# Gated cross-attention and mixture-of-experts block on one core: table scatters issued one by one, row statistics moved between the heads, and Wq's low parts made between GpSimd's additions

## The chip, the cores and the metric

One core of a Trainium2 chip runs the whole program in one launch. The metric is device microseconds of one execution.

## What is computed

Cut to what matters (16 sequences of 112 rows, width 512, context of 375 rows of 128; 16 heads; 64 experts, 8 chosen per row):

```python
def attention(hidden_q, kv_c):                     # kv_r = rope(kv_c)
    q_big = einsum(hidden_q @ Wq.T, w_kc_q)        # per head: 512 -> 128 -> 384
    q_big = rope(q_big)
    scores = (q_big @ W_qr) @ (kv_r @ W_kr).T      # softmax over 375
    return concat(softmax(scores) @ kv_r @ w_kc_kv) @ Wo.T

def experts(x):
    topv, topi = top_k(x @ gate_w.T, 8)
    out = sum of softmax(topv) * dp_w[e] @ (silu(gate_e(x)) * up_e(x)) over the 8 experts e
    return out + sigmoid(x @ sh_gate1_w.T) * shared_expert(x)

x = x + tanh(g_xattn) * attention(layernorm(x), ctx)
x = x + tanh(g_ffn) * experts(layernorm(x))
```

## The kernel before

**Stages.** W_qr and W_kr are first folded into one matrix per head (`m_w`), and w_kc_kv and Wo into another (`v_w`). The 16 sequences ("batches") are then taken in 4 groups of 4 (`GB = 4`, `NG = 4`, 448 rows). Each group has a head phase, an attention phase and an output product (`project_out`). Behind the last group come the steps of the last batches (`END`), the loop over 64 experts, and the sum of the parts.

**A head phase** is a loop over h = 0 to 17, one pass per head and two passes of tail. Pass h has this work, for head h unless another is named:

- PE: `project` (12 matmuls, x by Wq's high and low parts, bank 0), `latent` of head h-1 (9 matmuls, banks 1 to 4), `to_context` of head h-2 (3 products in fp32, 6 rows in the trace, L680, bank 5).
- ACT: copies out the high parts, `q_hk..h` (L1321) and `q_th` (L1331).
- DVE: subtracts the low parts, `q_hk..l` (L967) and `q_tl` (L990), and between them `latent` of head h-1: seven rope products (L980 and L984), of which four belong to the chunks c = 0 and 1.
- GpSimd (POOL): three additions `q_rope <- q_rope, q_sin` of head h-1 (L1542), chunks c = 0, 1, 2. The first two wait for DVE's fourth rope product, the third for the seventh.

PE's `project` of head n waits for the low part of `q_hk` of head n-1, and `to_context` of n waits for `q_tl` of n-1 (one bank each).

**Wq's split.** In the first head phase alone (g = 0) the weights are also split: ACT makes the high part of Wq for head h+1 and of w_kc_q for head h, POOL the low parts (`split_wq`, L1530, and `split_wcq`, L1536). `project` of head n then waits for `s_wq_lo >= n + 1`, the end of `split_wq(n)`. `split_wq(1)` is issued in pass 0, `split_wq(h + 1)` in pass h. Later groups load both parts from memory.

**The steps between the heads.** For groups 1 to 3, the feed-forward preparation of the four batches of the group before is spread over the slots of the head phase: an even slot 2h lies behind `latent` of pass h, an odd slot 2h+1 behind `to_context`. A table (`SLOTS`, `PERIOD = 7`, `between`) gives each step of batch i of the group the slot 7i plus an offset. The steps are: "norm" (DVE, L1109, waits for POOL's inverse root), "turn" (transposes on PE, L769), "router" (PE L749, DVE L1054 to L1057), "choose" (DVE, top 8 and their weights, L1062 to L1081), "rank" (PE), "place" (DVE, eight expert positions per row, L1087 to L1099; PE L791), "shared" (DVE, L1131 to L1135), and "scatter low" and "scatter high": four indirect DMAs each on POOL (L1561) that write one entry of the table per row and choice. SP's stores follow 4 slots behind (`STORE_LAG`).

**Row statistics.** `project_out` of a group ends on DVE with, per batch, the residual addition (L1039), `bn_stats` (L1044) and `bn_aggr` (L1046), and on POOL with two small instructions that make the inverse root (`spread`, L1522 and L1524).

Every engine executes its own list in order; no scheduler stands between.

Of the kernel before, what the change touches and what calls it, by code (L numbers as in the profile page):

```python
# [18 lines left out]
H, K, Q, R = 16, 128, 384, 64  # L19
E, I, TOP = 64, 128, 8  # L20
# [4 lines left out]
QC = 3  # L25
# [4 lines left out]
GB = 4  # L30
NG = B // GB
# [69 lines left out]
HALF = GB // 2 * RT + ALL_LAGS  # L101
PASSES = [tuple(range(g * GB, (g + 1) * GB)) for g in range(NG - 1)] + [(B - 4, B - 3), (B - 2, B - 1)]
STEPS = ("norm", "turn", "router", "choose", "rank", "place", "shared", "scatter low", "scatter high")
SLOTS = (0, 4, 6, 7, 9, 10, 11, 11, 12)
PERIOD, STORE_LAG = 7, 4
NR = 23
R_LOGIT, R_VALUE, R_SHARED, R_MASK, R_SHIFT, R_RANKED, R_COUNT, R_POS = 1, 2, 3, 7, 9, 15, 16, 20
NF, NO, NX, NW, NV, NP = 6, 4, 8, 2, 4, 4
# [2 lines left out]
CT = B * S // P  # L111


def between(g, slot):
    if g == 0:
        return []
    return [(step, (g - 1) * GB + i) for i in range(GB) for at, step in zip(SLOTS, STEPS) if PERIOD * i + at == slot]


LATE = {HALF + 2 + n * 3 // 2: (STEPS[n % len(STEPS)], B - GB + n // len(STEPS)) for n in range(2 * len(STEPS))}  # L120
# [47 lines left out]
def build(nc, a, out):  # L168
    with ExitStack() as ctx:
# [62 lines left out]
        x_sb = [sb(f"x_sb{i}", [S, C]) for i in range(NX)]  # L232
# [11 lines left out]
        ln_stats = [sb(f"ln_stats{i}", [S, 16]) for i in range(GB + 1)]  # L244
# [671 lines left out]
        def vector(dve):  # L916
# [105 lines left out]
            def keep_context(b, blk):  # L1022
# [2 lines left out]
                dve.tensor_tensor(q_rows(1, b, blk * TB * P, width), bank[5 + n % 2][:, 0:width],  # L1025
                                  q_rows(0, b, blk * TB * P, width), ALU.subtract).then_inc(s_ctx_lo, 1)

            def project_out(p):
                for h in range(H):
                    n = p * H + h  # L1030
                    high, low = v_w[n % 2]
                    dve.wait_ge(s_v_hi, n + 1)
                    dve.tensor_tensor(low[:], v_raw[n % NV][:], high[:], ALU.subtract).then_inc(s_v_lo, 1)  # L1033
                for b in PASSES[p]:
                    x, st = x_sb[b % NX], ln_stats[b % GB]
                    dve.wait_ge(s_o, (p + 1) * H)
                    if b == 0:
                        dve.wait_ge(s_tanh, 1)
                    dve.scalar_tensor_tensor(x[:], bank[4 + b % GB][0:S, :], tanh_g[0:S, 0:1], x[:], ALU.mult, ALU.add)\  # L1039
                       .then_inc(s_x2, 1)  # L1040
                    dve.wait_ge(s_x2, b + 1)
                    if b >= GB:
                        dve.wait_ge(s_nm2, b - GB + 1)
                    dve.bn_stats(st[:, 0:6], x[:]).then_inc(s_bn2, 1)  # L1044
                    dve.wait_ge(s_bn2, 2 * b + 1)
                    dve.bn_aggr(st[:, 6:8], st[:, 0:6]).then_inc(s_bn2, 1)  # L1046

            def router_out(b, bk):
                at = NR * b
# [50 lines left out]

            def finish(step, b, bk):
                at = NR * b
                if step == "norm":
                    st = ln_stats[b % GB]
                    if b:
                        dve.wait_ge(s_xn2_st, 16 * b)
                        dve.wait_ge(s_x2tr, b)
                    dve.wait_ge(s_rs2, 2 * (b + 1))
                    dve.tensor_scalar(xn2[:], x_sb[b % NX][:], st[:, 6:7], st[:, 0:1], ALU.subtract, ALU.mult)\  # L1109
                       .then_inc(s_nm2, 1)  # L1110
                if step in ("router", "router out"):
                    router_out(b, bk)
                if step == "choose":
                    choose(b)
                if step == "place":
                    place(b)
                if step == "order":
                    dve.wait_ge(s_total, 1)
                    dve.tensor_copy(total[:], bank[3][0:E, 0:E]).then_inc(s_ranked, 1)
                    dve.tensor_tensor(key_own[:], bank[3][0:E, 0:1], lower_own[:], ALU.add).then_inc(s_ranked, 1)  # L1120
                    dve.tensor_tensor(key[:], bank[3][0:E, E:2 * E], lower_first[:], ALU.add).then_inc(s_ranked, 1)
                    dve.wait_ge(s_ranked, 3)
                    dve.tensor_scalar(above[:], key[:], key_own[:], 0.0, ALU.is_gt, ALU.add, accum_out=place_of[:])\
                       .then_inc(s_ranked, 1)
                    dve.wait_ge(s_ranked, 4)
                    dve.tensor_scalar(at_place[:], expert[0:E, :], place_of[:], None, ALU.is_equal).then_inc(s_ranked, 1)
                    dve.wait_ge(s_total, 2)
                    dve.tensor_copy(order[:], bank[4][0:1, 0:E]).then_inc(s_order, 1)
                if step == "shared":
                    dve.wait_ge(s_sh, 4 * (b + 1))  # L1130
                    dve.tensor_scalar(small[:, 1:2], small[:, 0:1], 1.0, 0.5, ALU.add, ALU.mult).then_inc(s_route, 1)  # L1131
                    dve.wait_ge(s_route, at + R_POS + 1)
                    dve.tensor_tensor(small[:, 2:3], small[:, 1:2], tanh_g[0:S, 1:2], ALU.mult).then_inc(s_route, 1)
                    dve.wait_ge(s_route, at + R_POS + 2)
                    dve.scalar_tensor_tensor(x_sb[b % NX][:], bank[bk][0:S, :], small[:, 2:3], x_sb[b % NX][:],  # L1135
                                             ALU.mult, ALU.add).then_inc(s_route, 1)
# [18 lines left out]
            for h in range(1, H, 2):  # L1155
                n = H + h
# [362 lines left out]
        def gpsimd(pool):  # L1519
            def spread(st, s_bn, s_rs, b):  # L1520
                pool.wait_ge(s_bn, 2 * (b + 1))
                pool.tensor_scalar(st[:, 0:1], st[:, 7:8], EPS, None, ALU.add).then_inc(s_rs, 1)  # L1522
                pool.wait_ge(s_rs, 2 * b + 1)
                pool.tensor_tensor(st[:, 0:1], st[:, 0:1], minus_half[0:S, :], ALU.pow).then_inc(s_rs, 1)  # L1524

            def split_wq(n):
                if n < H:
                    high, low = wq_s[n % 2]
                    pool.wait_ge(s_wq_hi, n + 1)
                    pool.tensor_tensor(low[:], wq[n % NW][:], high[:], ALU.subtract).then_inc(s_wq_lo, 1)  # L1530

            def split_wcq(n):
                if n < H:
                    high, low = wcq_s[n % 2]
                    pool.wait_ge(s_wcq_hi, n + 1)
                    pool.tensor_tensor(low[:], wcq[n % NW][:], high[:], ALU.subtract).then_inc(s_wcq_lo, 1)  # L1536

            def latent(n):
                o = q_rope[n % 2]
                for c in range(QC):  # L1540
                    pool.wait_ge(s_rope, ROPES * n + (4, 4, 7)[c])
                    pool.tensor_tensor(o[:, c, :], o[:, c, :], q_sin[:, c, :], ALU.add).then_inc(s_radd, 1)  # L1542

# [5 lines left out]
                        .then_inc(s_scaled["pool"], 1)  # L1549

            def project_out(p):
                for b in PASSES[p]:
                    spread(ln_stats[b % GB], s_bn2, s_rs2, b)

            def finish(step, b):
                half = {"scatter low": range(TOP // 2), "scatter high": range(TOP // 2, TOP)}.get(step, ())
                for k in half:
                    if k % (TOP // 2) == 0:
                        pool.wait_ge(s_route, NR * b + R_POS)
                        pool.wait_ge(s_zero, 32)  # L1560
                    pool.indirect_dma_start(table, bass.IndirectOffsetOnAxis(ap=pos_i[b % 2][:, k:k + 1], axis=0),  # L1561
                                            entry[b % 2][:, k, :], None).then_inc(s_tab[b % 2], 16)
# [5 lines left out]
            for g in range(NG):  # L1568
                for h in range(H + 2):
                    if h < H:  # L1570
                        split_wcq(g * H + h)
                        split_wq(g * H + h + 1)
                    if 1 <= h <= H:
                        latent(g * H + h - 1)
                    for step, b in between(g, 2 * h):
                        finish(step, b)
                    for step, b in between(g, 2 * h + 1):
                        finish(step, b)
                for t in range(GB * RT + ALL_LAGS):
                    if g == NG - 1 and t == HALF:  # L1580
                        project_out(NG - 1)
                    if g == NG - 1 and LATE.get(t):
                        finish(*LATE.get(t))
                    if 0 <= t - 2 < GB * RT:
                        normalise(g * GB * RT + t - 2)
                    if t < GB * RT:
                        b, i = g * GB + t // RT, t % RT
                        if i == 2 and b + GB < B:
                            spread(ln_stats[GB], s_bn1, s_rs1, b + GB)
                project_out(g if g < NG - 1 else NG)  # L1590
# [90 lines left out]
```

## Time and profile before

| | |
|---|---|
| median of 3 runs | 1776.56 us (1768.63 to 1781.8) |
| profiled execution | 1785.47 us, its span 1783.7 us |
| mean granted TensorE clock | 0.925 of full |
| PE / DVE / ACT / POOL busy, share of the span | 82% / 70% / 40% / 48% |
| first head phase (g = 0) | 76.1 to 199.8 us |
| head phases of groups 1, 2, 3 | 344.9 to 492.7, 637.9 to 785.8, 931.2 to 1079.2 us |

In the rows of the timeline the first number is the start in microseconds, the second the duration; "idle before" in brackets is the time that the engine had nothing running ahead of the row, with what ended it. Rows of several instructions carry "x3". PE's matmuls overlap, so starts are compared, not durations. In the table of stretches the third column from the end is the clock that TensorE was granted, 1.00 for 2.4 GHz and 0.50 for 1.2 GHz.

### The profile page before, as it was taken

To read this page: it belongs to the slowest core of one execution; us is meant where nothing else is said; L and a number is where in the kernel's file an instruction comes from. 1 tells how busy PE (TensorE), PEld (TensorE's weight loads), DVE (VectorE), ACT (ScalarE), POOL (GpSimd) and SP (SyncE) were. 2 spreads that over 40 slices of the span, in tenths; PEclk is the share of its full clock that TensorE was granted. 3 is DMA by queue.
4 is the path that set the end of the run, shared out by engine and by line. 5 is a ranking of instruction groups with operands and counts; after the bars stand their busy time and mean duration, and the time that the engine had idled before them with its cause. 6 is when DMAs were issued, how large, how long until landed. Compare 5 with 4: busy or idle time off the path is not lost. (4 is left out here: it accounts for less than half of the span.)

```text
span 1783.7 us, 24623 instructions
## 1 busy us (share of the span) xinstructions
PE 1456.5 (82%) x7484; PEld 1170.1 (66%) x7484; DVE 1253.4 (70%) x2658; ACT 711.6 (40%) x1605; POOL 857.6 (48%) x901
## 2 busy tenths in 40 slices
PE   4689898899889989979899988988479898898600
PEld 3367687676578776658777666665268788888500
DVE  2268796389889358979737897675457677777577
ACT  1123475111167311127611115554157677677400
POOL 1078552056655025655404656221377777777500
PEclk9989999999999999989999998999689999999855
DMA  6977300354310235420034530302278899999798
GB/s 189 321 234 245 102 14 26 102 157 142 104 44 6 67 121 153 141 76 18 16 113 134 137 108 15 88 28 77 74 217 265 303 322 320 305 304 295 253 425 353
DMA packets 140412, 286.01 MB, mean 160 GB/s; under 512 B 29422, under 2 KB 64840, under 8 KB 138184
## 3 DMA queue, kind: packets, MB, share of 16 engines
q1 hardware_dynamic: 112328, 212.39, 37.2%
q0 software_dynamic: 25344, 64.69, 11.0%
q10 hardware_dynamic: 2608, 7.34, 1.4%
q8 instruction: 62, 1.02, 0.3%
q14 instruction: 70, 0.57, 0.1%
HBM read 218.90 MB, written 67.61 MB: 161 GB/s over the span
## 5 line engine op out<-in xcount | busy, mean ns | idle before, releaser
L1542 POOL TENSOR_TENSOR q_rope<-q_rope,q_sin 128x448 f32<-128x448 f32 x192 | 214.7, 1148 | 158.9 <-DVE q_sin L984 158.6
L1548 POOL TENSOR_TENSOR prob<-prob,row_inv 128x375 f32<-128x375 f32 x201 | 162.5, 812 | 137.3 <-DVE row_inv L1006 137.2
L680 PE MATMUL bank<-q_rope,m_w 128*128 128x448 f32 x384 | 170.7, 581 | 32.4 <-DVE q_tl L990 20.4
L1608 POOL DMA_INDIRECT parts<-y_sb,t_rows x140 | 155.0, 1107 | 51.5 <-issue 35.4
L1561 POOL DMA_INDIRECT table<-entry,pos_i x128 | 121.6, 950 | 103.9 <-DVE pos_i L1099 57.8
L1601 POOL DMA_INDIRECT x_g<-xn_dram,t_rows x140 | 142.8, 1020 | 50.5 <-issue 40.2
L984 DVE TENSOR_TENSOR q_sin<-bank,sin_q 128x448 f32<-128x448 f32 (+1 forms) x256 | 158.4, 619 | 3.9
L1340 ACT ACTIVATE prob<-bank,row_max 128x375 f32<-128x375 f32 x224 | 128.6, 574 | 40.8 <-DVE row_max L998 40.4
L705 PE MATMUL bank<-ident,prob 128*125 128x128 f32 x672 | 119.6, 289 | 26.9 <-POOL prob L1548 9.4
L680 PEld LDWEIGHTS bank<-q_rope,m_w 128*128 128x128 f32 x384 | 75.6, 203 | 98.9 <-issue 91.8
L998 DVE TENSOR_REDUCE row_max<-bank 128x1 f32<-128x375 f32 x224 | 119.5, 534 | 24.1 <-PE bank L604 23.4
L705 PEld LDWEIGHTS bank<-ident,prob 128*125 128x125 f32 x672 | 103.1, 194 | 47.8 <-POOL prob L1548 30.4
L1522 POOL TENSOR_SCALAR ln_stats<-ln_stats 112x1 f32<-112x1 f32 x32 | 7.4, 232 | 256.1 <-DVE ln_stats L1046 223.8
L1331 ACT ACTIVATE q_th<-bank 128x448 fp32r<-128x448 f32 x64 | 34.7, 542 | 222.9 <-PE bank L680 222.9
L980 DVE TENSOR_TENSOR q_rope<-bank,cos_q 128x448 f32<-128x448 f32 x192 | 118.1, 615 | 0.0
L1495 ACT ACTIVATE y_sb<-bank,t_rows 112x512 f32<-112x512 f32 (+2 forms) x140 | 91.3, 685 | 14.1 <-PE bank L604 13.9
L602 PE MATMUL bank<-xg_t1h,w_gu_s1h 128*128 128x224 f32 (+2 forms) x256 | 75.6, 295 | 23.3 <-DVE e_half L1245 23.2
L866 PE MATMUL bank<-ident,x_g 112*128 112x112 f32 (+2 forms) x560 | 66.6, 265 | 33.2 <-DMA x_g<-xn_dram,t_rows 33.2
L866 PEld LDWEIGHTS bank<-ident,x_g 112*128 112x128 f32 (+2 forms) x560 | 60.6, 144 | 44.0 <-DMA x_g<-xn_dram,t_rows 35.9
L1235 DVE TENSOR_TENSOR w_gu_s1l<-w_gu,w_gu_s1h 128x1024 fp32r<-128x1024 f32 x32 | 39.3, 1228 | 52.0 <-ACT w_gu_s1h L1478 51.9
L602 PE MATMUL bank<-xg_t0h,w_gu_s0h 128*128 128x224 f32 (+2 forms) x256 | 74.9, 292 | 1.1 <-DVE e_half L1245 0.8
L1033 DVE TENSOR_TENSOR v_w0l<-v_raw,v_w0h 128x512 fp32r<-128x512 f32 x40 | 27.7, 692 | 68.4 <-ACT v_w0h L1371 68.0
(277 smaller groups left out, 4526.6 us busy)
## 6 DMA issues: line engine op xcount, KB each, us to landing
w_gu<-in_w_gu SPq DMA_DIRECT2D x64, 512.0 KB, 4.8
p_in<-parts SPq DMA_DIRECT2D x14, 2304.0 KB, 13.1
v_raw<-v_dram SPq DMA_DIRECT2D x80, 256.0 KB, 2.7
w_dp<-in_w_dp SPq DMA_DIRECT2D x64, 256.0 KB, 6.0
m_w<-m_dram SPq DMA_DIRECT2D x64, 192.0 KB, 2.7
wq_s0h<-wq_dram SPq DMA_DIRECT2D x24, 256.0 KB, 3.5
wq_s0l<-wq_dram SPq DMA_DIRECT2D x24, 256.0 KB, 3.6
wq_s1h<-wq_dram SPq DMA_DIRECT2D x24, 256.0 KB, 3.1
```

Source lines behind the costliest of these rows:

```text
L602: pe.matmul(out_ap, wh, mh, start=first, stop=False)
L680: m = pe.matmul(bank[5][:, 0:GT], m_w[n % NW][:, c, :], q_rope[h % 2][:, c, :], start=(c == 0), stop=(c == QC - 1))
L705: m = pe.transpose(bank[bk][0:LP, j * P:(j + 1) * P], prob[n % NP][:, j * LP:(j + 1) * LP], ident[:])
L866: m = pe.transpose(bank[n % 3][:, j * size:(j + 1) * size], x_g[x % NXE][0:size, t, j * P:(j + 1) * P], ident[0:size, 0:size])
L984: dve.tensor_tensor(q_sin[to:to + size, other, :].rearrange("p (b s) -> p b s", b=GB), src[at:at + size], table, ALU.mult).then_inc(s_rope, 1)
L998: dve.tensor_reduce(row_max[:, i:i + 1], bank[n % 3][:, 0:L], AX_X, ALU.max, negate=True).then_inc(s_max, 1)
L1340: act.activation(prob[i][:], bank[n % 3][:, 0:L], ACT.Exp, bias=row_max[:, i:i + 1], accum_out=row_sum[:, i:i + 1]).then_inc(s_exp, 1)
L1542: pool.tensor_tensor(o[:, c, :], o[:, c, :], q_sin[:, c, :], ALU.add).then_inc(s_radd, 1)
L1548: pool.tensor_tensor(prob[i][:], prob[i][:], row_inv[:, i:i + 1].to_broadcast([P, L]), ALU.mult)\
L1561: pool.indirect_dma_start(table, bass.IndirectOffsetOnAxis(ap=pos_i[b % 2][:, k:k + 1], axis=0), entry[b % 2][:, k, :], None).then_inc(s_t ...
L1601: pool.indirect_dma_start(x_g[x % NXE][0:size, t, :], None, xn2_dram, bass.IndirectOffsetOnAxis(ap=t_rows[x % NROW][0:size, t, 0:1].bitcas ...
L1608: pool.indirect_dma_start(parts, bass.IndirectOffsetOnAxis(ap=t_rows[x % NROW][0:size, t, 1:2].bitcast(I32), axis=0), y_sb[x % NY][t][0:si ...
```

## The change

It has three parts. (1) `SLOTS` becomes the function `slots(i)` with period 8: every step keeps one parity for all batches ("choose", "rank", "norm" and "shared" odd, "turn", "router", "place" even), and the eight scatters get eight steps, one per slot (for the last batch three per slot). (2) `bn_stats`, `bn_aggr` and POOL's `spread` leave `project_out` for the first three groups and become a step "stats", one slot ahead of each batch's "norm". (3) In pass h POOL issues the additions c = 0 and 1 of head h-1 ahead of `split_wq(h + 1)` and the addition c = 2 behind it.

```diff
-SLOTS = (0, 4, 6, 7, 9, 10, 11, 11, 12)
-PERIOD, STORE_LAG = 7, 4
+PERIOD, STORE_LAG = 8, 4
+SCATTERS = {"scatter low": range(TOP // 2), "scatter high": range(TOP // 2, TOP),
+            **{f"scatter {k}": range(k, k + 1) for k in range(TOP)}}
...
+def slots(i):
+
+    at = PERIOD * i
+    last = i == GB - 1
+    return {"stats": max(0, at - 2), "norm": max(1, at - 1), "turn": at + 2, "router": at + 4, "choose": at + 5,
+            "rank": at + 7, "place": at + 8, "shared": at + 9,
+            **{f"scatter {k}": at + 9 + (k // 3 if last else k) for k in range(TOP)}}
...
-    return [(step, (g - 1) * GB + i) for i in range(GB) for at, step in zip(SLOTS, STEPS) if PERIOD * i + at == slot]
+    return [(step, (g - 1) * GB + i) for i in range(GB) for step, at in slots(i).items() if at == slot]
...
                     dve.scalar_tensor_tensor(x[:], bank[4 + b % GB][0:S, :], tanh_g[0:S, 0:1], x[:], ALU.mult, ALU.add)\
                        .then_inc(s_x2, 1)
-                    dve.wait_ge(s_x2, b + 1)
-                    if b >= GB:
-                        dve.wait_ge(s_nm2, b - GB + 1)
-                    dve.bn_stats(st[:, 0:6], x[:]).then_inc(s_bn2, 1)
-                    dve.wait_ge(s_bn2, 2 * b + 1)
-                    dve.bn_aggr(st[:, 6:8], st[:, 0:6]).then_inc(s_bn2, 1)
+                    if p >= NG - 1:
+                        stats_x2(b)
...
+                if step == "stats":
+                    stats_x2(b)
...
             def project_out(p):
-                for b in PASSES[p]:
+                if p >= NG - 1:
+                    for b in PASSES[p]:
+                        spread(ln_stats[b % GB], s_bn2, s_rs2, b)
...
+                if step == "stats":
                     spread(ln_stats[b % GB], s_bn2, s_rs2, b)
...
                     if h < H:
                         split_wcq(g * H + h)
+                    if 1 <= h <= H:
+                        latent(g * H + h - 1, range(QC - 1))
+                    if h < H:
                         split_wq(g * H + h + 1)
                     if 1 <= h <= H:
-                        latent(g * H + h - 1)
+                        latent(g * H + h - 1, range(QC - 1, QC))
```

`stats_x2(b)` is the five removed lines (`bn_stats` and `bn_aggr` with their waits) as a function. The last group's steps (`LATE`, `END`) keep the nine old steps.

POOL in passes 1 to 3 of the first head phase, before. `wq_s..l` is the low part of Wq that `project` reads, `wcq_s..l` that of w_kc_q, and the numbers 0 and 1 are the two buffers:

```order
L1536 TENSOR_TENSOR wcq_s1l<-wcq,wcq_s1h 128x384
L1530 TENSOR_TENSOR wq_s0l<-wq,wq_s0h 128x512
L1542 TENSOR_TENSOR q_rope<-q_rope,q_sin 128x448 x3
L1536 TENSOR_TENSOR wcq_s0l<-wcq,wcq_s0h 128x384
L1530 TENSOR_TENSOR wq_s1l<-wq,wq_s1h 128x512
L1542 TENSOR_TENSOR q_rope<-q_rope,q_sin 128x448 x3
```

The same passes in the changed kernel:

```order
L1553 TENSOR_TENSOR wcq_s1l<-wcq,wcq_s1h 128x384
L1559 TENSOR_TENSOR q_rope<-q_rope,q_sin 128x448 x2
L1547 TENSOR_TENSOR wq_s0l<-wq,wq_s0h 128x512
L1559 TENSOR_TENSOR q_rope<-q_rope,q_sin 128x448
L1553 TENSOR_TENSOR wcq_s0l<-wcq,wcq_s0h 128x384
L1559 TENSOR_TENSOR q_rope<-q_rope,q_sin 128x448 x2
L1547 TENSOR_TENSOR wq_s1l<-wq,wq_s1h 128x512
L1559 TENSOR_TENSOR q_rope<-q_rope,q_sin 128x448
```

Two additions of head h-1 now stand between the low part of w_kc_q and the low part of Wq for head h+1.

DVE at the end of the first group's `project_out` and the start of the next head phase, before (`x_sb` is the residual row block of a batch, `xn` its normalised copy):

```order
L1039 SCALAR_TENSOR_TENSOR x_sb<-bank,tanh_g,x_sb 112x512
L1044 BN_STATS ln_stats<-x_sb 112x6
L1046 BN_AGGR ln_stats<-ln_stats 112x2
L967 TENSOR_TENSOR q_hk0l<-bank,q_hk0h 128x448
L1109 TENSOR_SCALAR xn<-x_sb,ln_stats 112x512
L967 TENSOR_TENSOR q_hk1l<-bank,q_hk1h 128x448
```

(these are the last of four such triples) and in the changed kernel:

```order
L1058 SCALAR_TENSOR_TENSOR x_sb<-bank,tanh_g,x_sb 112x512 x4
L977 TENSOR_TENSOR q_hk0l<-bank,q_hk0h 128x448
L1043 BN_STATS ln_stats<-x_sb 112x6
L1045 BN_AGGR ln_stats<-ln_stats 112x2
L1126 TENSOR_SCALAR xn<-x_sb,ln_stats 112x512
L977 TENSOR_TENSOR q_hk1l<-bank,q_hk1h 128x448
```

The first head's low part moved ahead of all statistics; those of the other three batches stand in passes 3, 7 and 11.

POOL in the head phase of group 1, before, from pass 5:

```order
L1561 DMA table<-entry,pos_i 131072x3 x4
L1542 TENSOR_TENSOR q_rope<-q_rope,q_sin 128x448 x3
L1561 DMA table<-entry,pos_i 131072x3 x4
L1542 TENSOR_TENSOR q_rope<-q_rope,q_sin 128x448 x9
L1561 DMA table<-entry,pos_i 131072x3 x8
```

and in the changed kernel, passes 6 and 7 with the odd slot of pass 5 ahead:

```order
L1580 DMA table<-entry,pos_i 131072x3 x2
L1559 TENSOR_TENSOR q_rope<-q_rope,q_sin 128x448 x3
L1580 DMA table<-entry,pos_i 131072x3 x2
L1559 TENSOR_TENSOR q_rope<-q_rope,q_sin 128x448 x3
L1580 DMA table<-entry,pos_i 131072x3
L1539 TENSOR_SCALAR ln_stats<-ln_stats 112x1
L1541 TENSOR_TENSOR ln_stats<-ln_stats,minus_half 112x1
L1580 DMA table<-entry,pos_i 131072x3
```

No pass has more than two scatters now, and the inverse root of the third batch stands behind three additions and one scatter.

## Rows read from the trace of the kernel before

**Rows 1.** Stretches: length, busy time of five engines, granted clock, DMA share, GB/s
```profile
104.50:182.50 78.00, 78.00 (x327) 61.00 (x325) 61.30 (x108) 24.23 (x48) 66.59 (x61) 1.00 0.73 234
344.90:492.70 147.80, 129.87 (x509) 94.81 (x507) 124.52 (x260) 22.49 (x56) 84.07 (x85) 0.94 0.43 128
```
**Rows 2.** Timeline, one steady pass of the first head phase, all four engines
```profile
117.53 0.71 PE L602 MATMUL bank<-xn_th,wq_s1h 128*128 128x448 f32 x1
120.50 0.54 ACT L1321 ACTIVATE q_hk1h<-bank 128x448 fp32r<-128x448 f32 x1 [0.95 <-PE bank L604]
121.72 1.27 POOL L1530 TENSOR_TENSOR wq_s0l<-wq,wq_s0h 128x512 fp32r<-128x512 f32 x1
123.21 0.61 DVE L984 TENSOR_TENSOR q_sin<-bank,sin_q 128x448 f32<-128x448 f32 x1
123.91 3.39 POOL L1542 TENSOR_TENSOR q_rope<-q_rope,q_sin 128x448 f32<-128x448 f32 x3 [0.91 <-DVE q_sin L984]
124.02 0.71 PE L602 MATMUL bank<-xn_th,wq_s0h 128*128 128x448 f32 x1
```
**Rows 3.** Timeline, POOL and PE where the third and fourth heads' products start, and the last
```profile
95.53 0.71 PE L602 MATMUL bank<-xn_th,wq_s0h 128*128 128x448 f32 x1 [11.04 <-POOL wq_s0l L1530]
96.42 3.34 POOL L1542 TENSOR_TENSOR q_rope<-q_rope,q_sin 128x448 f32<-128x448 f32 x3 [0.99 <-DVE q_sin L984]
104.53 0.71 PE L602 MATMUL bank<-xn_th,wq_s1h 128*128 128x448 f32 x1
182.46 0.71 PE L602 MATMUL bank<-xn_th,wq_s1h 128*128 128x448 f32 x1
```
**Rows 4.** Waits of PE in the head phase of group 1: total, times, longest
```profile
PE bank L680 <- DVE q_tl L990: 5.1, 1, 5.1
PE bank L602 <- DVE q_hk0l L967: 4.7, 1, 4.7
PE bank L680 <- issue: 3.2, 2, 1.8
PE bank L769 <- DVE rank_sb L1087: 2.4, 2, 1.7
PE bank L680 <- POOL q_rope L1542: 0.9, 1, 0.9
```
**Rows 5.** Timeline, start of that phase on DVE, ACT and PE
```profile
345.09 0.75 DVE L1039 SCALAR_TENSOR_TENSOR x_sb<-bank,tanh_g,x_sb 112x512 f32<-112x512 f32 x1 [4.12 <-PE bank L604]
347.52 0.54 ACT L1321 ACTIVATE q_hk0h<-bank 128x448 fp32r<-128x448 f32 x1 [7.28 <-PE bank L604]
351.45 0.59 DVE L967 TENSOR_TENSOR q_hk0l<-bank,q_hk0h 128x448 fp32r<-128x448 f32 x1
352.18 0.71 PE L602 MATMUL bank<-xn_th,wq_s1h 128*128 128x448 f32 x1 [4.70 <-DVE q_hk0l L967]
```
**Rows 6.** Stretch behind that wait, columns as in rows 1
```profile
352.00:357.00 5.00, 4.82 (x13) 4.34 (x14) 0.49 (x2) 0.00 (x0) 0.53 (x1) 0.50 0.01 3
```
**Rows 7.** Timeline, "choose" and the products behind it in two places of that phase
```profile
376.71 0.23 DVE L1068 TENSOR_TENSOR mask<-left,logit 112x64 f32<-112x64 f32 x1
406.68 3.37 POOL L1542 TENSOR_TENSOR q_rope<-q_rope,q_sin 128x448 f32<-128x448 f32 x3
407.63 2.51 DVE L1068 TENSOR_TENSOR mask<-left,logit 112x64 f32<-112x64 f32 x1
412.71 3.93 PE L680 MATMUL bank<-q_rope,m_w 128*128 128x448 f32 x6 [1.81 <-issue]
```
**Rows 8.** Timeline, "place" of the first batch, a scatter, and the phase's last product
```profile
389.46 0.23 DVE L1087 TENSOR_TENSOR rank_sb<-bank,expert_entries 112x64 f32<-112x64 f32 x1
393.11 0.62 DVE L990 TENSOR_TENSOR q_tl<-bank,q_th 128x448 fp32r<-128x448 f32 x1
436.01 0.94 POOL L1561 DMA_INDIRECT table<-entry,pos_i  x1 [0.30 <-issue]
487.22 4.19 PE L680 MATMUL bank<-q_rope,m_w 128*128 128x448 f32 x6 [5.07 <-DVE q_tl L990]
```

More of the change, by code:

```diff
@@ L1026, in keep_context, with stats_x2 @@
                                   q_rows(0, b, blk * TB * P, width), ALU.subtract).then_inc(s_ctx_lo, 1)
+            def stats_x2(b):
+                st = ln_stats[b % GB]
+                dve.wait_ge(s_x2, b + 1)
+                if b >= GB:
+                    dve.wait_ge(s_nm2, b - GB + 1)
+                dve.bn_stats(st[:, 0:6], x_sb[b % NX][:]).then_inc(s_bn2, 1)
+                dve.wait_ge(s_bn2, 2 * b + 1)
+                dve.bn_aggr(st[:, 6:8], st[:, 0:6]).then_inc(s_bn2, 1)
             def project_out(p):
@@ L1034, in project_out @@
                 for b in PASSES[p]:
-                    x, st = x_sb[b % NX], ln_stats[b % GB]
+                    x = x_sb[b % NX]
                     dve.wait_ge(s_o, (p + 1) * H)
@@ L1536, in split_wcq, with latent @@
                     pool.tensor_tensor(low[:], wcq[n % NW][:], high[:], ALU.subtract).then_inc(s_wcq_lo, 1)
-            def latent(n):
+            def latent(n, chunks):
                 o = q_rope[n % 2]
-                for c in range(QC):
+                for c in chunks:
                     pool.wait_ge(s_rope, ROPES * n + (4, 4, 7)[c])
@@ L1551, in project_out, with finish @@
             def project_out(p):
-                for b in PASSES[p]:
+                if p >= NG - 1:
+                    for b in PASSES[p]:
+                        spread(ln_stats[b % GB], s_bn2, s_rs2, b)
+            def finish(step, b):
+                if step == "stats":
                     spread(ln_stats[b % GB], s_bn2, s_rs2, b)
-            def finish(step, b):
-                half = {"scatter low": range(TOP // 2), "scatter high": range(TOP // 2, TOP)}.get(step, ())
-                for k in half:
+                for k in SCATTERS.get(step, ()):
                     if k % (TOP // 2) == 0:
```

## The prediction

> **What bounds the kernel now.** I read the table of stretches first, to see which engine fills each phase. In the first head phase, from the fourth head's product to the last, PE is busy in all 78.0 us and the clock is at its upper level, 2.4 GHz [rows 1]. Twelve passes take these 78 us, 6.5 us each [rows 3], and that is PE's own work. In the head phase of group 1 PE is busy in 129.9 of 147.8 us and DVE in 124.5 [rows 1]: both near full, so a wait of either is seen in the end time. The timeline of one pass comes second, since it shows who hands what to whom [rows 2]; then the waits of PE in group 1, which name 16.3 us of idle time [rows 4], and the timeline at the places where they end [rows 5, 7, 8]. The reader is to see in the first that POOL's split of Wq (start 121.72) ends at 122.99, 1.0 us before the product that needs it starts at 124.02: this is all the slack there is.
>
> **Wq's split behind two additions.** It touches the first head phase alone, where PE is the bound and the split has 1.0 us to spare. In pass h POOL now makes the additions c = 0 and 1 of head h-1 first. They wait for DVE's fourth rope product, which ends at 123.82 [rows 2]. That product stands on DVE behind the low part of q_hk of head h, which needs ACT's copy, which needs PE's `project` of head h. And `project` of head h+1 waits for the split. So a chain through PE, ACT, DVE and POOL closes from one `project` to the next, where before it was open. Its length from rows 2, from the start of `project` at 117.53:
>
> - to ACT's copy, 120.50: 2.97 us; from there through ACT, DVE's low part and four rope products to POOL's first addition at 123.91: 3.41. Together 6.38, with every wait on it already a wait for its predecessor.
> - two of three additions, 3.39 x 2/3 = 2.26 us, and the split, 1.27: 9.91.
> - the hand-over to PE, about 0.1, as between DVE's fourth product (ended 123.82) and POOL's start: 10.0 us.
>
> A pass is thus 10.0 us in place of 6.5, and PE idles 3.5 us in each. The third addition comes 1.3 us later, which nobody waits for: its reader on PE stands behind the next `project` and `latent`. DMA load falls, since the same bytes move in longer passes.
>
> What the idle time does to the clock: behind a wait of 4.70 us [rows 5] the twelve matmuls of `project` ran from 352.18 to about 357.0 at 0.50, 1.2 GHz [rows 6], against 2.97 us until ACT could start at 2.4 GHz: some 2.0 us more. The L680 product behind a wait of only 1.81 us took 3.93, and that behind 5.07 took 4.19 [rows 7, 8]. `project` of the next head stands right behind each idle 3.5 us and is on the chain. The ends are 0 and 2.0 us per pass, and 12.0 for the pass; a slow `latent` might add 0.2. The rows with waits on both sides of 3.5 us are slow, so I take two passes in three: 1.35, and 11.35 us per pass.
>
> The first case is the third head's product. POOL can start its additions at 96.42 [rows 3]; two of them are 2.23 and the split 1.27: PE starts at 100.0 instead of 95.53, +4.5. It then runs at half clock as before, so the pass to the fourth head is 12.0 instead of 9.0 (95.53 to 104.53), +3.0. Twelve passes follow: 12 x (11.35 - 6.5) = 58.2. Sum +65.7 us, with ends 4.5 + 3.0 + 12 x 3.5 = 49.5 and 4.5 + 3.0 + 12 x 5.7 = 75.9.
>
> **Statistics out of `project_out`.** The four triples and the wait behind them fill DVE from 345.09 to 351.45, 1.59 us per batch, of which the addition is 0.75. Without the rest DVE is done at about 348.0, and ACT's copy of the first q_hk is ready at 348.06 (347.52 + 0.54) [rows 5]. DVE's low part then starts at 348.1 instead of 351.45: 3.35 us gained. PE's wait shrinks from 4.70 to 1.35, and the half clock of that product may go; I count half of its 2.0, 1.0 us. What is late next is this same copy. The price is in the phase: `bn_stats` and `bn_aggr` take 0.84 us on DVE per batch as before, but "norm" in the odd slot waits for POOL's inverse root, and in passes 7 and 11 this stands behind three additions (3.4 us from DVE's fourth product on) and one scatter (0.94 and 0.30 between two) [rows 8]. Behind DVE's wait stand the next q_hk low part and the whole next `latent`. No row of before shows it; the ends are 0 (DVE has slack in passes without steps, 78.0 - 61.3 over 12 passes [rows 1]) and the additions' tail plus scatter plus root, about 3. I take 0.9 for the second batch, which has no scatter ahead, and 2.2 each for the third and fourth: -5.3.
>
> **Period 8 and single scatters.** "choose" now always stands behind `q_tl`. Before, in two batches it stood ahead of it, and beside POOL's additions: the mask took 2.51 us instead of 0.23, ending when the three additions ended (406.68 + 3.37) [rows 7], and PE waited for `q_tl` 1.8 and 1.4 us, the 3.2 that the view calls issue [rows 4]. "turn" no longer meets the "place" of the batch before: 2.4. No run of eight scatters (1.24 us each) stands ahead of additions: 0.9. Sum 6.5 us per phase, and half clock behind the 3.2: about 1.6. Against this, "place" stands ahead of `q_tl` in all four batches, not in two. It holds it up by 3.65 us (389.46 to 393.11) [rows 8]. In the middle this is partly covered by the two passes that PE may lag; at the end it is not: before the last product (487.22) DVE had only "shared", about 1.1 us, ahead of `q_tl`, and now "place": -2.5. The ends of this part are a loss of 3 (PE waits at all four) and a gain of 8. Issuing a scatter costs the same 0.94 us wherever it stands, and 8 of the last batch still run behind the last addition.
>
> The Trainium skill ("SBUF — State Buffer", Who interferes with whom) says that a DVE instruction with two SBUF inputs contends with a GpSimd one that reads SBUF, and one fully blocks; the mask in rows 7 agrees. The page also holds that DVE's two-port copies lock GpSimd out of writing descriptors, which would speak against scatters spread beside "choose": by that rule they would lengthen by a copy of some 0.2 us each, under 3 us in all, and the sum would be the same within its bounds. No run here shows it yet.
>
> Group sum: 3.35 + 1.0 - 5.3 + 6.5 + 1.6 - 2.5 = 4.65 gained, about 5, with ends -3 and +11; times 3 phases 15 us, ends -9 and +33.
>
> **Sum.** +65.7 - 15 = +51 on the profiled execution of 1785.5 us: 1836. The median of the runs shown is 1776.6, 9 us below the profiled one, and the terms are differences, so the forecast for a median is 1776.6 + 51 = 1827 us.
>
> **The rivals.**
>
> A. The chain closes, but the clock stays at 2.4 GHz. For it: a wait of 1.7 us ("rank_sb") left no slow product that PE's wait list shows. Against: rows 6 to 8. Then +49.5 - 15 = +34: 1811.
>
> B. The chain closes, and the phases of groups 1 to 3 gain nothing, since DVE's waits for POOL and "place" ahead of `q_tl` eat the rest. For it: DVE is busy in 124.5 of 147.8 us. Then +65.7: 1842.
>
> C. Faster. All idle time of PE in the three later phases goes, 16.3 us each, with the half-clock cost behind it (2.0 + 1.8 + 1.8 + 1.8, from 4.82 and 4.19 us against full clock): up to 24 x 3 = 71 us, against the cheap end of the chain, 49.5: 1755. It decides from 49.5 / 3 = 16.5 us per phase on. Against it: "place" ahead of the last `q_tl` leaves the longest wait standing.
>
> D. The change doesn't do what it says, because PE's `project` doesn't wait for the split in time: this would be so if POOL ran a pass ahead. Rows 3 speak against it, with PE released by exactly this split at 95.53. Then only the group term is left, -15: 1762.
>
> **How the numbers follow.** Forecast 0.66, A 0.16, B 0.12, C 0.03, D 0.03. The forecast's own range is 1776.6 + (7.5 + 12 x 4.0 - 20) = 1812 to 1776.6 + (75.9 - 5) = 1847. With A's lower bounds the range of 8 in 10 is 1802 to 1848. A measurement of this kernel can tell about 1% from no change: 1794 and above is slower. All of the forecast and B, and nearly all of A, lie there: slower 0.93. C and D less their near parts are faster by over 1%: 0.03; within 1%: 0.04.
>
> **What would show it.** In the changed profile, PE's waits in the first head phase should name POOL's `wq_s..l`, some 14 times and 3 to 4 us each, and the phase should be about 65 us longer, with a granted clock well under 1.00. Starts of `project` 10 to 12 us apart there are the step itself; 6.5 would make it wrong. In group 1 the second `project` should start 3.9 us behind the first, not 7.3, DVE's "norm" should show waits of 1 to 2 us for POOL's root, the mask should be at 0.23, and the last product should still wait about 5 us for `q_tl`. Later phases longer than 147.8 us would make the gain wrong.

## The result, and the profile after

| | before | after |
|---|---|---|
| median (4 runs each) | 1776.47 us | 1814.31 us (1812.33 to 1816.43) |
| ratio after / before | | 1.0207, 95% interval 1.0178 to 1.0236 |
| span of the profiled execution | 1783.7 us | 1810.9 us |
| mean granted clock | 0.925 | 0.923 |
| first head phase, first product to first score | 75.89 to 201.16: 125.3 us | 75.76 to 257.79: 182.0 us |
| head phases of groups 1, 2, 3, likewise | 147.9, 148.4, 148.5 us | 141.1, 138.9, 138.8 us |

The change costs 2.1%. The first head phase is 56.7 us longer, and the three later ones are 25.9 us shorter together. With the attention phases between them (1.5 us less), the last group's first score comes 29.2 us later (1079.74 to 1108.92), and the profiled spans are 27.2 us apart. What follows that score is the same code in all these kernels (but for the last experiment's), and took 694 to 705 us in their profiled executions. The medians are 37.8 us apart. Of the 9 us between 29.2 and 37.8 no phase shows anything. They lie within that spread, and the profiled execution of before was itself 9 us above its median; where they arise stays open.

Stretches of the changed kernel (columns as in rows 1): a short pass of the first head phase, a long one, twelve passes, and the head phase of group 1.

```profile
110.80:120.50 9.70, 6.77 (x28) 5.05 (x28) 5.16 (x9) 2.02 (x4) 5.57 (x6) 0.98 0.50 164
120.50:131.50 11.00, 8.10 (x27) 6.15 (x28) 5.15 (x9) 2.02 (x4) 5.46 (x6) 0.86 0.45 143
110.82:239.04 128.22, 95.21 (x325) 71.95 (x325) 61.84 (x108) 23.68 (x47) 66.11 (x61) 0.87 0.45 146
400.60:541.70 141.10, 126.50 (x509) 93.59 (x508) 119.13 (x260) 22.76 (x56) 85.60 (x85) 0.95 0.44 133
```

Twelve passes took 78.0 us with PE busy in all of them [rows 1]. Now they take 128.22, PE is busy in 95.21, and the clock is 0.87. The busy time of DVE (61.84) and POOL (66.11) is that of before: nothing became more work, the engines wait for each other. The timeline of two passes shows in which order:

```profile
110.82 0.44 PE L612 MATMUL bank<-xn_th,wq_s1h 128*128 128x448 f32 x1 [2.91 <-issue]
113.52 0.54 ACT L1338 ACTIVATE q_hk1h<-bank 128x448 fp32r<-128x448 f32 x1 [4.10 <-PE bank L614]
116.93 2.22 POOL L1559 TENSOR_TENSOR q_rope<-q_rope,q_sin 128x448 f32<-128x448 f32 x2 [4.13 <-DVE q_sin L994]
119.11 1.25 POOL L1547 TENSOR_TENSOR wq_s0l<-wq,wq_s0h 128x512 fp32r<-128x512 f32 x1
120.47 0.71 PE L612 MATMUL bank<-xn_th,wq_s0h 128*128 128x448 f32 x1 [2.91 <-issue]
124.56 0.55 ACT L1338 ACTIVATE q_hk0h<-bank 128x448 fp32r<-128x448 f32 x1 [5.50 <-PE bank L614]
127.97 2.22 POOL L1559 TENSOR_TENSOR q_rope<-q_rope,q_sin 128x448 f32<-128x448 f32 x2 [5.54 <-DVE q_sin L994]
131.51 0.44 PE L612 MATMUL bank<-xn_th,wq_s1h 128*128 128x448 f32 x1 [2.91 <-issue]
```

This is the closed chain: product, ACT's copy 2.70 us later, POOL's two additions 3.41 us behind that, the split, the next product. The first pass is 9.65 us. The second is 11.04, and the whole difference (1.39) lies between PE's start and ACT's copy, 4.09 against 2.70: the product ran the first eight of its twelve matmuls at half clock (0.57 us each, then 0.36). The view of PE's waits for the same phase, and for group 1's:

```profile
PE bank L612 <- issue: 35.9, 13, 2.9
PE bank L612 <- POOL wq_s0l L1547: 15.2, 1, 15.2
...
PE bank L690 <- DVE q_tl L1000: 6.4, 1, 6.4
PE bank L690 <- issue: 5.5, 3, 2.3
PE bank L612 <- DVE q_hk0l L977: 1.4, 1, 1.4
```

The 35.9 us in 13 waits are the chain, though the view names no releaser; only the timeline shows that each ends 0.1 us behind POOL's split. In group 1 the wait for `q_hk0l` has shrunk from 4.7 to 1.4 us and the `rank_sb` waits are gone [rows 4]. The two waits called issue (1.8 and 1.4 us, 3.2 in rows 4) have made way for three others of that name, 1.0 and twice 2.3. DVE and PE in that phase, in order of time:

```profile
406.26 0.55 DVE L1126 TENSOR_SCALAR xn<-x_sb,ln_stats 112x512 f32<-112x512 f32 x1 [1.00 <-POOL ln_stats L1541]
428.74 0.55 DVE L1126 TENSOR_SCALAR xn<-x_sb,ln_stats 112x512 f32<-112x512 f32 x1 [0.98 <-POOL ln_stats L1541]
451.31 0.22 DVE L1083 TENSOR_TENSOR mask<-left,logit 112x64 f32<-112x64 f32 x1
461.17 0.55 DVE L1126 TENSOR_SCALAR xn<-x_sb,ln_stats 112x512 f32<-112x512 f32 x1 [2.18 <-POOL ln_stats L1541]
470.67 3.85 PE L690 MATMUL bank<-q_rope,m_w 128*128 128x448 f32 x6 [2.25 <-issue]
495.31 0.55 DVE L1126 TENSOR_SCALAR xn<-x_sb,ln_stats 112x512 f32<-112x512 f32 x1 [2.16 <-POOL ln_stats L1541]
530.54 2.48 DVE L1103 TENSOR_TENSOR count<-count,mask 112x64 f32<-112x64 f32 x1
535.89 4.49 PE L690 MATMUL bank<-q_rope,m_w 128*128 128x448 f32 x6 [6.37 <-DVE q_tl L1000]
```

"norm" waits for POOL's inverse root in all four batches; the mask takes 0.22 to 0.27 us in all four; and the last product still waits, 6.37 us, and then takes 4.49 us, where one at full clock takes 2.49.

### The profile page after: what moved, and what is told of

The parts are those of the page before. It is cut to its first block and busy times, and to the rows that moved or that the text cites. A ratio compares the mean times of both kernels' runs of the same rounds, so it can differ in the third digit from the quotient of the medians.

```text
span 1810.9 us, 24623 instructions
## 1 busy us (share of the span) xinstructions
PE 1460.4 (81%) x7484; PEld 1174.9 (65%) x7484; DVE 1238.3 (68%) x2658; ACT 711.2 (39%) x1605; POOL 858.7 (47%) x901
## 5 line engine op out<-in xcount | busy, mean ns | idle before, releaser
L690 PE MATMUL bank<-q_rope,m_w 128*128 128x448 f32 x384 | 166.4, 572 | 38.0 <-DVE q_tl L1000 21.3
L612 PE MATMUL bank<-xn_th,wq_s0h 128*128 128x448 f32 x128 | 56.7, 443 | 31.8 <-issue 16.5
L612 PE MATMUL bank<-xn_th,wq_s1h 128*128 128x448 f32 x128 | 57.7, 450 | 24.9 <-issue 19.4
```

The lines of the kernel that those rows point to most:

```text
L612: pe.matmul(out_ap, wh, mh, start=first, stop=False)
L690: m = pe.matmul(bank[5][:, 0:GT], m_w[n % NW][:, c, :], q_rope[h % 2][:, c, :], start=(c == 0), stop=(c == QC - 1))
```

## Experiments

**The split's part alone, and the rest without it.** Before with part (3) only:

```diff
                     if h < H:
                         split_wcq(g * H + h)
+                    if 1 <= h <= H:
+                        latent(g * H + h - 1, range(2))
+                    if h < H:
                         split_wq(g * H + h + 1)
                     if 1 <= h <= H:
-                        latent(g * H + h - 1)
+                        latent(g * H + h - 1, range(2, QC))
```

> The kernel before with part 3 alone: POOL makes two additions ahead of the split of Wq. Theory (the split closes a chain from one project to the next): the first head phase from first product to first score grows from 125.3 to about 182 us as in the changed kernel, the later phases stay at 147.9 to 148.5, and the time is before + 56 us, about 1832. Rival (the loss comes from the steps between the heads, scatters one by one beside DVE's work; the split is hidden): before within 5 us, 1772 to 1782.

Measured: 1839.12 us, 1.035 of before (1.0315 to 1.0385). The first head phase took 183.0 us, the others those of before (148.0, 148.4, 147.8). The changed kernel with its POOL order of before (parts 1 and 2 only):

> The changed kernel with part 3 undone: statistics between the heads, period 8, single scatters. Theory: passes of 6.5 us in the first head phase again, 139 to 141 us in the three later ones, together 26 us less than before: about 1751. Rival (the split is hidden, the loss is in the slots): as the changed kernel, about 1814.

Measured: 1753.45 us, 0.9857 (0.9828 to 0.9887), first phase 126.7 us, later ones 140.9 to 141.2. The two parts, +63.2 and -22.5 us by their medians, add up to 40.7 against 37.8 for both. The loss is the split's; without it the change is a gain.

From group 1 on, part (3) changes nothing, since nothing is split there: this run and the changed kernel have the same instructions in the same order in these phases. Yet groups 2 and 3 took 141.2 us here and 138.9 and 138.8 there. So a difference of 2 us in a phase is not yet an effect.

**One and three additions ahead of the split.** The same edit with `range(1)` and `range(3)`, one run each.

> The kernel before with one addition, not two, ahead of Wq's split. Theory: the chain is shorter by one addition of 1.12 us, so the mean pass of the first head phase is 10.7 - 1.1 = 9.6 us if the clock behaves the same, and its end some 43 us later than before. Rival (any addition ahead costs the same, because the waits of PE are for a store or a buffer, not for POOL's queue): 10.7 us.

> The kernel before with all three additions ahead of Wq's split. Theory: one addition of 1.12 us more than in the changed kernel, a pass of 11.8 us; the third addition waits for DVE's seventh product, which is done by then. Rival (waits for a store or a buffer): 10.7 us.

Twelve passes with one, with two (the split alone, above) and with three additions ahead of the split:

```profile
108.61:211.55 102.94, 80.97 (x325) 59.96 (x325) 61.81 (x109) 24.14 (x48) 66.56 (x61) 1.00 0.56 182
```
```profile
111.89:239.73 127.84, 94.06 (x324) 70.98 (x325) 61.77 (x108) 23.70 (x47) 66.15 (x61) 0.88 0.46 146
```
```profile
114.42:259.73 145.31, 100.04 (x324) 76.05 (x325) 61.77 (x108) 23.68 (x47) 65.89 (x61) 0.85 0.40 129
```

| additions ahead | pass | PE idle in it | clock | chain at full clock: 9.65 less or plus 1.11 |
|---|---|---|---|---|
| 0 (before) | 6.5 us | 0 | 1.00 | open |
| 1 | 8.58 | 1.83 | 1.00 | 8.54 |
| 2 (changed kernel) | 10.69 | 2.75 | 0.87 | 9.65 |
| 3 | 12.11 | 3.77 | 0.85 | 10.76 |

The first addition costs 2.1 us a pass, since it closes the chain; each further one costs its 1.11 and what the clock adds. The rival, 10.7 us whatever the number, is out. With one ahead I had expected passes of 9.6 us, at least partly at half clock, and the phase's end some 43 us later: missed. The clock never fell, and the end came 27.6 us later (228.7 against 201.2; the run took 1809.85 us). With two additions the product was slow in 8 of 12 passes, with three in all 12 (11.8 us a pass expected, 12.11 measured; the run took 1860.22 us). In the run with one addition the view of PE's waits names ACT's copy of a high part of Wq. But this copy belongs to the other buffer and ends 0.73 us ahead of the product, while POOL's split ends 0.1 us ahead of it, as in the changed kernel.

**Another split behind the same two additions.** Before, with POOL's order Wq's low part, additions c = 0 and 1, w_kc_q's low part, addition c = 2:

```diff
                     if h < H:
-                        split_wcq(g * H + h)
                         split_wq(g * H + h + 1)
                     if 1 <= h <= H:
-                        latent(g * H + h - 1)
+                        latent(g * H + h - 1, range(QC - 1))
+                    if h < H:
+                        split_wcq(g * H + h)
+                    if 1 <= h <= H:
+                        latent(g * H + h - 1, range(QC - 1, QC))
```

> The kernel before, with the two additions put ahead of the other split instead: POOL's order in a pass is Wq's low part, additions c = 0 and 1, w_kc_q's low part, addition c = 2. The reader of w_kc_q's low part is latent of head h, which stands on PE behind the next project. By the same reading of rows 2 another chain closes: from latent's first matmul (about 120.2) to POOL's first addition (123.91) 3.7 us, two additions 2.26, the split 0.95, the hand-over 0.1: 7.0 us from one latent to the next, against 6.5 of PE's own work. So passes of about 7.0 us, idle pieces of PE of only 0.5 us, and a clock that stays at its upper level: the first head phase is 6 to 9 us longer. Rival: any split behind additions costs as much as Wq's (passes of 9.6 us or more); or this one costs nothing (6.5 us), since its reader comes later.

```profile
126.48 0.44 PE L602 MATMUL bank<-q_hk1h,wcq_s1h 128*128 128x448 f32 x1 [0.26 <-issue]
```

Measured: passes of 7.0 and 6.5 us in turn, 6.76 on average, with a wait of 0.27 us at every second `latent`, clock 1.00; the phase 5.4 us longer (130.7 against 125.3), a little under the 6 to 9 expected, since only every second pass is held up: from the start of `latent` to POOL's first addition it takes 3.60 us in one pass (119.55 to 123.15), and 3.18 in the next, where `latent` starts behind the wait (126.48 to 129.66). (One run, 1775.61 beside 1783.44 of before: no verdict on the total.) What counts is not the two additions but when the split behind them is read.

**Statistics alone, slots alone.** First, "stats" moved, with period 7 and the old offsets for all other steps but "norm", which stands one slot earlier than before (its edit is shown). Second, period 8 with single scatters, the statistics left in `project_out`:

```diff
-SLOTS = (0, 4, 6, 7, 9, 10, 11, 11, 12)
+    return {"stats": max(0, at - 2), "norm": max(1, at - 1), "turn": at + 4, "router": at + 6, "choose": at + 7,
+            "rank": at + 9, "place": at + 10, "shared": at + 11, "scatter low": at + 11, "scatter high": at + 12}
```

> The kernel before with the statistics alone moved between the heads (period 7, old slots, scatters in fours, no change to Wq's split). The prediction's sum for this part was 3.35 + 1.0 - 5.3, a loss of 0.95 us per phase, 3 in all: 1779 us. Theory now, after the changed kernel's trace: the start of a phase gains about 4.7 us (the first q_hk low part no longer waits, and the product behind it runs at full clock). With a period of 7 only the norms of batches 0 and 2 stand in odd slots, right behind POOL's additions, and wait 1.0 and some 2.2 us. The gain is 1.5 to 4 us per phase, 5 to 12 in all: 1764 to 1771 us, phases of 144 to 146 us in place of 148. Rival: the statistics carry nearly the whole gain of the group phases (7 us each): 1755.

> The kernel before with the slots alone changed (period 8, parity kept, single scatters), the statistics left in the output product and Wq's split as before. The prediction's sum for this part was 6.5 + 1.6 - 2.5 = 5.6 us gained per phase: 1759 to 1760 us. Theory: without norms that wait for POOL, PE should show the gap of some 4.7 us at the phase's start again, with half clock behind it, and none of 2.3 us in the middle: phases of 142 to 144 us, 1760 plus or minus 4. Rival: the slots give little and the statistics nearly all: 1770 or more. If parts do not add up, the two savings of this and of the run with statistics alone will differ from the 23 us that both gave together.

Measured: statistics alone 1786.22 us, 1.0052 (1.0025 to 1.0078), phases of 150.3 to 150.4 us: half a per cent slower, where I had expected 1764 to 1771. Slots alone 1746.69 us, 0.9811 (0.9775 to 0.9847), phases of 137.6 to 137.8 us, where I had expected 1760 and 142 to 144. By the phases this is better than both parts together: shorter than all six of the changed kernel and the run without the split's part (138.8 to 141.2). By the totals alone it isn't shown, as the intervals of 0.9811 and 0.9857 overlap. The two changes of the total, +7.4 and -32.1 us, nearly add up to the -22.5 of both. With the statistics alone, POOL and DVE around the third batch's norm:

```profile
391.28 3.36 POOL L1557 TENSOR_TENSOR q_rope<-q_rope,q_sin 128x448 f32<-128x448 f32 x3
394.80 0.94 POOL L1578 DMA_INDIRECT table<-entry,pos_i  x1 [0.17 <-issue]
396.05 0.94 POOL L1578 DMA_INDIRECT table<-entry,pos_i  x1 [0.30 <-issue]
397.30 0.94 POOL L1578 DMA_INDIRECT table<-entry,pos_i  x1 [0.30 <-issue]
398.54 0.94 POOL L1578 DMA_INDIRECT table<-entry,pos_i  x1 [0.30 <-issue]
399.85 0.57 POOL L1539 TENSOR_TENSOR ln_stats<-ln_stats,minus_half 112x1 f32<-112x1 f32 x1
```
```profile
400.56 0.55 DVE L1124 TENSOR_SCALAR xn<-x_sb,ln_stats 112x512 f32<-112x512 f32 x1 [6.24 <-POOL ln_stats L1539]
```

The inverse root stands behind three additions and a run of four scatters, and DVE waits 6.24 us for it, and 4.61 for the fourth batch's; my expectation had looked at the slots' parity and not at the scatters on POOL. With the slots alone, PE's waits in group 1 are the last and the first of the phase and the hand-over to the scores, nothing in the middle, and PE is busy in 118.60 of the 118.71 us from the second product to the last wait; before, in 123.10 of 129.98:

```profile
PE bank L690 <- DVE q_tl L1000: 6.3, 1, 6.3
PE bank L612 <- DVE q_hk0l L977: 4.7, 1, 4.7
PE bank L612 <- issue: 1.3, 1, 1.3
```
```profile
351.64:470.35 118.71, 118.60 (x490) 90.33 (x490) 106.42 (x235) 21.14 (x53) 73.18 (x69) 0.98 0.52 149
```
```profile
352.18:482.16 129.98, 123.10 (x490) 90.95 (x490) 112.29 (x237) 20.86 (x53) 73.46 (x70) 0.95 0.46 136
```

**Scatters in two fours again**, in the version without the split's part:

```diff
-            **{f"scatter {k}": at + 9 + (k // 3 if last else k) for k in range(TOP)}}
+            "scatter low": at + 9, "scatter high": at + 10}
```

> The changed kernel without its Wq part, with the scatters in two steps of four again (in the slots of the first and second single ones). Theory: a scatter costs POOL the same 0.94 us wherever it stands, but one of them stands ahead of the inverse root that the norms of batches 2 and 3 wait for. With fours none stands there, and these two waits shrink from 2.2 to about 1.0 us. So 1753 less 0 to 7: 1750, phases of 139 to 141 us. Rival: runs of four in front of the additions hold PE up as before (0.9 us per phase or more): 1756 or above, so single scatters are worth 3 us or more.

Measured: 1759.4 us, 0.9892 (0.9864 to 0.9919), phases of 142.1 to 143.1 us: the rival's side, though by little. The phases are longer than those same six, by 1 to 4 us; but the same code can differ by 2, and the interval of the total overlaps that without the split's part (0.9828 to 0.9887). What single scatters are worth is not settled by this. The norms wait only 0.98 us, as expected, but two of four masks are slow again, though "choose" kept its odd slot. POOL ahead of one, and DVE's row:

```profile
394.84 0.94 POOL L1578 DMA_INDIRECT table<-entry,pos_i  x1 [0.30 <-issue]
395.79 3.35 POOL L1557 TENSOR_TENSOR q_rope<-q_rope,q_sin 128x448 f32<-128x448 f32 x3
...
396.14 3.09 DVE L1081 TENSOR_TENSOR mask<-left,logit 112x64 f32<-112x64 f32 x1
```

Four scatters hold the additions up until they meet the mask, which then takes 3.09 us in place of 0.22, and ends 0.1 us behind the additions (399.14).

**Statistics one slot earlier**, also without the split's part:

```diff
-    return {"stats": max(0, at - 2), "norm": max(1, at - 1), "turn": at + 2, "router": at + 4, "choose": at + 5,
+    return {"stats": max(0, at - 3), "norm": max(1, at - 1), "turn": at + 2, "router": at + 4, "choose": at + 5,
```

> The changed kernel without its Wq part, with each batch's statistics one slot earlier, so that POOL's inverse root stands ahead of the pass's three additions and DVE's norm finds it done. Theory: the waits of 1.0, 2.2 and 2.2 us for POOL go; the two gaps of PE of 2.2 us in the middle of a phase go with them, and the clock stays at its upper level there. Gain up to 2 x 2.2 + 1.5 = 6 us per phase against 1753: 1735 to 1745, central 1740. Rival: DVE itself is the bound there (it is busy in over 90% of those passes), and the wait only moved; then 1750 to 1754.

Measured: 1737.35 us, 0.9776 (0.9754 to 0.9798), phases of 134.1 to 134.4 us, clock 1.00 from the second product to the last wait. PE's waits in group 1:

```profile
PE bank L690 <- DVE q_tl L1000: 6.3, 1, 6.3
PE bank L690 <- issue: 1.9, 3, 0.6
PE bank L612 <- DVE q_hk0l L977: 1.4, 1, 1.4
```

The inverse root now stands ahead of a pass's additions. Only the first batch's norm still waits (1.00 us), and each middle wait of PE fell to 0.6. It was POOL's order that held DVE, not DVE's load. The price is small: the three other norms start while POOL makes the additions and take 1.33 to 1.34 us, not 0.55. The one at 369.10 ends 0.3 us behind the additions.

**The last "place" behind the last `q_tl`**, on top of the earlier statistics, and then also the first probabilities off POOL:

```diff
-            "rank": at + 7, "place": at + 8, "shared": at + 9,
+            "rank": at + 7, "place": at + 8 + last, "shared": at + 9 + last,
```
```diff
-    if g == NG - 1 and HALF <= t:
+    if g and t < 8 or g == NG - 1 and HALF <= t:
```

> The run with earlier statistics, and in it the place and shared steps of each group's last batch one slot later, behind the last q_tl. Theory: place ahead of the last q_tl is what PE's last wait of 6.3 us per phase is made of, and the half clock of the product behind it (4.8 against 2.5 us): both go, 5 to 8 us less until the first score, phases of 127 to 130 us. But the eight scatters of that batch (1.24 us each) then still end at the same place, and POOL's normalisation of the first probabilities stands behind them, so most of it comes back in the attention phase: 1737 less 0 to 6, central 1734 us. Rival: the wait ends by itself and nothing on POOL matters: the full 3 x 7 = 20 us are gained, 1717.

> The same, and the first six probability tiles of groups 1 to 3 are normalised by ACT and DVE in turn, as the last group's later tiles already are, so that nothing of the start of an attention phase stands behind POOL's scatters. Theory: now the whole 5 to 7 us per phase are kept, less about 1 us of work more on ACT and DVE: 1737 less 10 to 18, central 1723 us. Rival: the first tiles are bound by DVE's row maxima and PE, not by POOL's scatters: no difference from the run before, 1731 to 1737.

Measured: 1732.56 us (0.9771, 0.9735 to 0.9807) and 1723.29 us (0.9704, 0.9673 to 0.9735). Both have phases of 129.2 to 129.3 us, 5 less than with the earlier statistics alone. PE's last wait for `q_tl` is 1.33 us in place of 6.3. In the first run PE then waits for POOL, whose normalisation stands behind eight scatters of the last batch (its slots hold three each, so the last passes have more than two); in the second that wait is 1.07 us:

```profile
463.64 2.89 PE L690 MATMUL bank<-q_rope,m_w 128*128 128x448 f32 x6 [1.33 <-DVE q_tl L1000]
```

```profile
478.64 1.00 PE L715 MATMUL bank<-ident,prob 128*125 128x128 f32 x3 [4.81 <-POOL prob L1565]
```
```profile
476.82 0.59 PE L715 MATMUL bank<-ident,prob 128*125 128x128 f32 x3 [1.07 <-DVE prob L1022]
```

Both totals fell as expected (1734 and 1723 us). But the first gained 15 us in its three phases and only 5 by its median, and as ratios to the runs of before the two are the same (0.9771 with it, 0.9776 without it): that this "place" alone pays is not shown by the total. I had expected the attention phases to take most of it back; the two that lie between head phases took 1.2 us each (147.3 against 146.1), and the rest isn't located. The last version beats both kernels, by 52 us (before) and 91 us (changed).

## Why the prediction was right, and where its sizes were off

Forecast 1827 us (1802 to 1848), measured 1814.31: slower, by the mechanism it named. The number alone doesn't say so, since rival A's 1811 lies nearer; the stretches and the experiments do.

- **The chain** closed as worked out. From the product to the additions it took 6.11 us, to the split 2.18, to the next product 1.36 (1.25 and 0.11): 9.65 in place of 10.0. Most of the difference is the first step. In rows 2 PE was busy up to the product, whose first matmul is 0.71 us long, and ACT's copy came 2.97 us behind its start; behind idle time these are 0.44 and 2.70. For the same reasons the signs were a little off: 13 waits of at most 2.9 us that the view calls issue, where some 14 of 3 to 4 us that name POOL were announced, and a phase 57 us longer, not 65.
- **The clock's price** was mis-sized, not its frequency. Two passes in three were named, and 8 of 12 were slow, but they took 10.85 to 11.82 us, some 1.5 over 9.65, not 2.0: per pass 1.0, not 1.35. The 2.0 had all twelve matmuls of `project` at half clock, as in rows 6; in the slow pass shown it was the first eight. That the frequency fits is luck in part: no row of before gave it, and with one addition it was 0 of 12, with three 12 of 12. With the third and fourth heads (+4.2 and +2.2, named +4.5 and +3.0) the first phase came out at +56.7 for +65.7.
- **Rival A** is refuted for two additions by the granted clock of 0.87, and would have held for one. **B** and **D** are refuted by the run without the split's part (0.9857, its phases 7 us shorter) and that with the split alone (+63.2 us). **C** counted on all idle time to go; the last wait stayed, as said against it.
- **The slots** were priced at 5.6 us per phase and gave 10.0, 10.7 and 10.8, outside my bound of 8. The waits named (6.5 us) were those that went (PE's idle time there 6.9 us before, 0.1 after). Two terms failed. One is the clock's: 1.6, where PE's busy time over the middle fell by 4.5 us (123.10 to 118.60, for 490 matmuls in both, at a clock of 0.95 and 0.98). The other is "place" at the end, named -2.5. The last wait was 6.3 us with the slots alone, and before it was 5.07 only in group 1, behind a product at half clock (4.19 us at 473.03); in groups 2 and 3 it was 6.55. So the new place cost nothing there. I had read group 1 alone, and only the stretch right ahead of `q_tl`: before, "place" stood at 478.38, ahead of the last head's rope products, and so on DVE's way to the last `q_tl` as well.
- **The statistics** were priced at -0.95 us and cost 3.1 to 3.5 per phase (140.9 to 141.2 against 137.6 to 137.8). In groups 2 and 3 of the changed kernel it was 1.1 to 1.3, so up to 2 us of this is no more than which products happened to run at half clock. DVE's waits were right to a tenth (0.9, 2.2, 2.2 named; 0.98, 2.18, 2.16 measured, and a fourth of 1.00 that was not named), and so was the gain at the start (3.3). The half clock behind the new waits was left out: 3.85 instead of 2.49 for the product at 470.67. The gain at the start was worth having only with the statistics one slot earlier: phases of 134.1 to 134.4 us against 137.6 to 137.8 (the totals, 1737.35 and 1746.69, have overlapping intervals).
- **"Choose" behind `q_tl`** was given as the reason for the fast mask. The run with scatters in fours shows that this is half of it: the additions must also start on time, and that takes the single scatters.
- **Rules.** The Trainium skill ("SBUF — State Buffer", Who interferes with whom) says that a DVE instruction with two SBUF inputs and a GpSimd one that reads SBUF exclude each other; the mask at 396.14 agrees (3.09 us for 0.22, ending with the additions). That scatters spread beside DVE's work lengthen by little held roughly: 105 of the changed kernel's 128 took 0.94 or 0.95 us, the others up to 1.35, against 121 of 128 and 1.24 before. That is some 3.5 us more in all, where under 3 were named.

Both sums erred toward a slower kernel, the loss 9 us too large and the gains 11 too small: by the trace the change is +30.8 us over the head phases where I had +51. By the medians it is +37.8, so part of how near 1827 came to 1814 is owed to some 7 us that no term of the sum holds.

## What to carry to other kernels

Before moving work ahead of an instruction on one engine, follow its result round all engines: if the work moved waits for something that in turn waits for this instruction's previous turn, an open pipeline becomes a closed loop, and the loop's length, not any engine's load, is the new pass. Put a short instruction that another engine waits for (here the inverse root) ahead of the long ones of its queue, a slot earlier than it is needed, and count everything between, asynchronous DMA issues too. When waits appear or go, price the clock on both sides. Before a wait is priced from one phase, compare it in the phases that repeat it.

## What was unexpected of the hardware

- The clock stood at 1.00 over twelve passes with 1.83 us of PE idle in each 8.58, and fell to 0.87 with 2.75 in each 10.69. The same wait also went either way: in the changed kernel the product behind 2.23 us of idle time ran at full speed in group 2 (2.49 us at 756.78), and behind 2.23 us in group 3 it did not (4.08 us at 1072.61). What decides between the two is open.
- What half clock cost differed with what it hit: 1.2 to 2.2 us on a pass of the chain, 1.4 to 2.0 us on one product of `to_context` (3.84 to 4.49 us instead of 2.49).
